# Local attention heads: the next job's first convolution laid between the logit turns, the softmax cut in three pieces

## The reference, cut to what matters

```
qkv = _conv1x1(xn, qkv_w, qkv_b).reshape(Bx, 3, HEADS, HD, Hx, Wx)
q, k, v = (qkv[:, 0], qkv[:, 1], qkv[:, 2])
...
qk = jnp.concatenate([(q * scale).reshape(Bx * HEADS, HD, Hx, Wx), k.reshape(Bx * HEADS, HD, Hx, Wx)], axis=1)
attn = jax.lax.conv_general_dilated(qk, dm_w, (1, 1), [(PAD, PAD), (PAD, PAD)], ...) + dm_b[None, :, None, None]
attn = attn.reshape(Bx, HEADS, K, Hx, Wx)
attn = attn + rel_bias.T[None, :, :, None, None]
attn = jax.nn.softmax(attn, axis=2)
...
out = jnp.einsum('bnckhw,bnkhw->bnchw', patches, attn).reshape(Bx, C, Hx, Wx)
```

## Time and profile before

| what | value |
|---|---|
| median of three runs | 5192.02 us |
| profiled execution: device time | 5200.72 us |
| profiled execution: span of the trace | 5198.9 us |
| PE busy | 4499.5 us (87%) |
| VectorE busy | 4251.0 us (82%) |
| POOL busy | 4077.5 us (78%) |
| ScalarE busy | 3168.0 us (61%) |
| first and last convolution matmul of the heads | 1308.2 to 2381.7 us |

### The profile page before, as it was taken

One profiled execution on the slowest core, in us unless ns is written; L12 is line 12 of the kernel. 1 busy time (PEld: TensorE's weight loads), 2 busy tenths in 40 slices (PEclk: granted clock), 3 DMA queues, 4 the chain that ended last, 5 costly groups with the idle time before them and its releaser, 6 DMA issues. The chain is left out here.

```text
span 5198.9 us, 68471 instructions
## 1 busy us (share of the span) xinstructions
PE 4499.5 (87%) x15210; PEld 2107.5 (41%) x15210; DVE 4251.0 (82%) x3462; ACT 3168.0 (61%) x6678; POOL 4077.5 (78%) x1926
## 2 busy tenths in 40 slices
PE   7998797986999999993788888889898888889897
PEld 2333463641666666662542323233232323232222
DVE  3776555554289999999559999999999999999995
ACT  5886565542011111110569888888888888888886
POOL 2544555544288988989659999999999999999993
PEclk9998998987999999996889999999999999999998
DMA  2000111327777777872428888788888888878883
GB/s 55 1 1 10 50 33 52 79 62 228 164 142 139 150 145 146 149 141 43 104 62 198 199 201 202 191 201 201 199 202 199 201 198 199 202 195 203 200 201 95
DMA packets 389221, 733.15 MB, mean 141 GB/s; under 512 B 78332, under 2 KB 119464, under 8 KB 375912
## 3 DMA queue, kind: packets, MB, share of 16 engines
q1 hardware_dynamic: 388968, 730.30, 60.3%
HBM read 594.31 MB, written 82.32 MB: 130 GB/s over the span
## 5 line engine op out<-in xcount | busy, mean ns | idle before, releaser
L2256 POOL TENSOR_TENSOR l_hc<-l_h,l_c_rep 128x1024 f32<-128x1024 f32 x768 | 1800.9, 2383 | 22.4 <-DVE l_h L2327 19.8
L1434 POOL TENSOR_TENSOR front<-l2b_v,front 128x1568 f32<-128x1568 f32 x276 | 936.9, 3463 | 235.4 <-ACT front L1395 119.0
L2327 DVE TENSOR_TENSOR_SCAN l_h<-l_p,l_h,l_bu 128x1024 f32<-128x1024 f32 x448 | 1026.3, 2328 | 5.3 <-ACT l_bu L2164 3.5
L2011 PE MATMUL l_p<-l_stacked,l_pick 96*128 96x512 f32 x1536 | 560.1, 446 | 224.3 <-DVE l_h L2327 204.9
L1482 DVE TENSOR_REDUCE l2b_osum<-front 128x32 f32<-128x1568 f32 x384 | 665.6, 1780 | 62.9 <-POOL front L1434 59.1
L2245 POOL TENSOR_TENSOR l_pool_bu<-l_du_rep,l_b_sb 128x1024 f32<-128x1024 f32 x256 | 610.7, 2386 | 39.7 <-DMA l_du_rep<-du_scratch 39.6
L2311 DVE TENSOR_TENSOR l_bu<-l_du_rep,l_p 128x1024 f32<-128x1024 f32 x512 | 610.8, 1193 | 25.7 <-DMA l_du_rep<-du_scratch 20.1
L1387 ACT ACTIVATE l2b_logits<-l2b_conv,l2b_this_b 98x512 f32<-98x512 f32 x96 | 66.1, 689 | 862.6 <-PE l2b_conv L1352 862.6
L2011 PEld LDWEIGHTS l_p<-l_stacked,l_pick 96*128 96x128 f32 x1536 | 242.8, 190 | 803.8 <-DVE l_h L2327 645.0
L2020 PE MATMUL l_p<-l_hc,l_y_pick 128*32 128x512 f32 x3072 | 522.1, 606 | 5.4 <-POOL l_hc L2256 5.4
L2327 DVE TENSOR_TENSOR_SCAN l_h<-l_p,l_h,l_pool_bu 128x1024 f32<-128x1024 f32 x224 | 523.2, 2336 | 3.6 <-ACT l_pool_bu L2164 2.3
(11 more groups left out here) (271 smaller groups left out, 8952.9 us busy)
## 6 DMA issues: line engine op xcount, KB each, us to landing
l_du_rep<-du_scratch SPq DMA_DIRECT2D x1536, 256.0 KB, 4.9
l2b_img_high<-qkv_scratch SPq DMA_DIRECT2D x192, 306.2 KB, 5.7
l2b_img_low<-qkv_scratch SPq DMA_DIRECT2D x192, 306.2 KB, 9.6
l_stacked<-l_parts SPq DMA_DIRECT2D x512, 96.0 KB, 3.3
l2b_v<-v_scratch SPq DMA_DIRECT2D x192, 152.0 KB, 6.4
qkv_scratch<-l2a_strip SPq DMA_DIRECT2D x32, 840.0 KB, 5.2
du_scratch<-l_du SPq DMA_DIRECT2D x128, 192.0 KB, 2.1
l_w_raw<-L_w_sed SPq DMA_DIRECT2D x32, 576.0 KB, 3.8
```

The lines of the kernel that those rows point to most:

```text
L1434: return eng.tensor_tensor(dst.rearrange("q x (dy dx) -> q x dy dx", dx=WIN), window, attn_half[:, :, unit % 2].rearrange("q x (dy dx) -> ...
L2011: pe.matmul(p_da[p % 2][:, e, :], pick[:, GRP[i] % (Q // DL), :], stacked[:, par, GRP[i] * DL // Q, :], start=True, stop=True).then_inc(s_ ...
L2256: pool.tensor_tensor(hc[:, slot:slot + 2, :], h[:, 2 * p:2 * p + 2, :], c_rep[:, par, :].unsqueeze(1).to_broadcast([128, 2, N]), ALU.mult) ...
L2327: dve.tensor_tensor_scan(flat(h[:, 2 * p:2 * p + 2, :]), flat(p_da[p % 2]), flat(of), state, ALU.mult, ALU.add).then_inc(s_h, 1)
```

## The change

`conv` is cut into three calls of a new `conv_pass`, one for each run of 14 matmuls. On PE the first chunk of job j+1 leaves the start of the next pass of the loop and goes between job j's turns: run 0, turns 0 to 2, run 1, turns 3 to 5, run 2, turns 6 and 7. Chunk 0 of job 0 goes ahead of the loop. The wait for the last logits stands behind run 0. On VectorE the softmax front is cut in the same three pieces, before units 26, 27 and 28. Nothing else is changed: SP, ScalarE and POOL run the same order of work, and no instruction of work is added or taken away.

```diff
-    SOFTMAX_AT = 26
+    SOFTMAX_AT = {26: (0, 1, 2), 27: (3, 4, 5), 28: (6, 7)}
...
+            PRODUCTS = ((0, 0), (1, 0), (0, 1))
+
+            def conv_pass(j, n, at, first=False):
+
+                b, ch = n // CHUNKS, n % CHUNKS
+                if at == 0:
+                    if ch == 0:
+                        pe.wait_ge(s_img[b % 2], 16 * 2 * SHIFTS * (B // 2) * j + 16 * 2 * SHIFTS * (b // 2 + 1))
+                    if not first:
+                        pe.wait_ge(s_log, j * JCHUNKS + (n - 1))
+                w_part, x_part = PRODUCTS[at]
+                for g in range(GROUPS):
+                    for dx in range(WIN):
...
+                if at == len(PRODUCTS) - 1:
+                    mm.then_inc(s_conv, 1)
+
             def conv(j, n, first=False):
...
+                for at in range(len(PRODUCTS)):
+                    conv_pass(j, n, at, first)
...
             def job(j, head, half, has_next, has_second):
                 first = isinstance(j, int) and j == 0
-                for n in range(JCHUNKS):
+                for n in range(1, JCHUNKS):
                     conv(j, n, first=first and n < 2)
-                pe.wait_ge(s_log, j * JCHUNKS + JCHUNKS)
-                for g in range(TURNS):
-                    turn(j, half, g, first=first and g < 3)
+                for at, groups in enumerate(SOFTMAX_AT.values()):
+                    if has_next:
+                        conv_pass(j + 1, 0, at)
+                    if at == 0:
+                        pe.wait_ge(s_log, j * JCHUNKS + JCHUNKS)
+                    for g in groups:
+                        turn(j, half, g, first=first and g < 3)
 
             pe.wait_ge(s_w, 64)
             pe.wait_ge(s_bias, 3)
+            conv(0, 0, first=True)
             all_jobs(job, pe)
...
-            def softmax(j, half):
-                for g in range(TURNS):
+            def softmax(j, half, groups):
+                for g in groups:
...
-                    if unit == SOFTMAX_AT and has_next:
-                        softmax(j + 1, 1 - half)
+                    if unit in SOFTMAX_AT and has_next:
+                        softmax(j + 1, 1 - half, SOFTMAX_AT[unit])
...
-            softmax(0, 0)
+            softmax(0, 0, range(TURNS))
```

More of the change, by code:

```diff
@@ L1340, in _ @@
         def _(pe):
-            def conv(j, n, first=False):
[L1343 to L1355, removed]
+            PRODUCTS = ((0, 0), (1, 0), (0, 1))
[9 more added lines that the diff above has]
+                    for dx in range(WIN):
+                        row = 2 * CP * ch + SHIFTS * g
+                        mm = pe.matmul(p_conv[n % 2][:], w_conv[w_part][:, g, dx, :],
+                                       img[x_part][:, b % 2, row:row + 2 * CP - 1:2, dx:dx + W],
+                                       start=(at == 0 and g == 0 and dx == 0),
+                                       stop=(at == len(PRODUCTS) - 1 and g == GROUPS - 1 and dx == WIN - 1))
+                if at == len(PRODUCTS) - 1:
+                    mm.then_inc(s_conv, 1)
+            def conv(j, n, first=False):
+                for at in range(len(PRODUCTS)):
+                    conv_pass(j, n, at, first)
             def turn(j, half, g, first=False):
```

## The result

| | before | after |
|---|---|---|
| median of four runs | 5191.84 us | 5227.28 us |
| profiled execution: device time | 5200.72 us | 5224.72 us |
| profiled execution: span | 5198.9 us | 5222.9 us |

The ratio is 1.0061, with a 95% interval of 1.0048 to 1.0075: 35.4 us slower between the medians. The prediction said 5223 us, between 5202 and 5252, and slower with a chance of 0.84.

What follows compares the result with a forecast made beforehand. PE's cycle set the pace, with the chain through SP's queue about 1 us from binding. Cycles +15.3, first job -2.4, clock +15, pieces +3 gave +31 us on 5192.0: 5223 us, range 5202 to 5252.

Steps and rivals of the forecast that it cites:

- The image's chain: VectorE, POOL, store, then load: image b=2 still lands 48.0 us after a job's first turn, unmoved by the change.
- PE's earlier arrival: PE reaches chunk 4 at 41.2 us after the first turn, was 49.2, so it newly waits 6.8 us for b=2.
- The cycle: First turn to next first turn: 91.85 us a job against 90.07, before clock and pieces are added.
- The clock: PE's granted clock falls in the idle ahead of chunk 4: 1.5 us a job, bounds 0 and 2.35.
- The pieces: VectorE's softmax cut in three meets the turns within 0.1 us: 0.3 us a job charged.
- VectorE's idle before its first maximum: Sign in the trace after: this idle up from 1 to 2 us to 4 to 5.
- First job: Job 0 has no store in the queue, so job 1 starts its turns 2.4 us early.
- Image b=0 as next in line: Load needed at 88.5 us after the first turn, estimated to land at 87: nothing charged, but next in line.
- the faster one: Rival: image b=2 in time for chunk 4, VectorE with POOL bind at 88.6 us a job: 5175 us, chance 0.08.
- Cold runs between the turns: Rival: transposes keep PE's clock low through runs 1 and 2, 3.36 us longer each: about 5290 us, chance 0.08.

Runs made afterwards that it cites:

- e3: Changed kernel with VectorE's softmax front whole again, in one piece before unit 26, PE's order as changed: 5258.14 us, ratio 1.0120 to the kernel before.
- e1: Changed kernel with the finished job's output store put behind image b=2 in SP's queue instead of ahead of it: 5205.08 us, ratio 1.0015 to the kernel before.
- e6: Changed kernel with SP's loads in the order their gates open, b=2 ahead of v's second half and the store, b=0 ahead of v's first half: 5174.69 us.
- e9: e6 with one move taken back, image b=0 behind v's first half again: 5218.94 us, ratio 1.0048 to the kernel before.
- e2: Kernel before the change with the output store put behind image b=2 in SP's queue: 5194.27 us, ratio 0.9996.
- e4: Changed kernel with 32 extra matmuls, result unused, on PE ahead of chunk 4's wait for image b=2: 5215.70 us, ratio 1.0035 to the kernel before.

## Why the prediction was right, point by point

- **The image's chain** (put at 48.0 us after the first turn, unmoved): chunk 4 started on it between 47.6 and 49.0, on average 48.3. Shown by the trace, by e3, which lengthens the chain by 2.9 us and the cycle with it, and by e1 and e6, which cut it and get 22 and 53 us back.
- **PE's earlier arrival** (41.2): 40.6, since three turns within the runs take 1.26 us of PE's time and not 1.6. The wait is thus 7.7 us on average instead of 6.8, the landing being 0.3 later as well; the earlier arrival makes the cycle no longer, as only the landing counts.
- **The cycle** (91.85 plus 1.8 for clock and pieces, 93.65): 94.0 us, from (2317.85 - 1471.48)/9 with the trace's first turns of jobs 1 and 10. From the first turn of job 1 to that of job 11 it is 938.4 us against 900.66: +37.7, where the sum had +33.3. The 4.4 us between them are the clock +6.4, the chain +2.8, the pieces -3 and the rest -1.8: the errors partly cancel, and that 5223 came so near 5227 is to that extent luck. The single distances are 92.9 to 95.5 us, a little wider than the 93 to 94 forecast.
- **The clock** (1.5 us a job, bounds 0 and 2.35): the term that was mis-sized most. Chunk 4 takes 1.4 to 2.8 us more than 10.07 after its wait, 2.1 on average over the ten. I had scaled it from the turns, in which PE was partly busy; a bare idle of 7 us costs more. The average lies within the upper bound, four single jobs over it. No row that I had read showed such an idle, but the trace of the kernel before has one, at the very first chunk of the heads, and it would have given 12.24 - 10.07 = 2.2:

```profile
1308.21 5.67 PE L1352 MATMUL l2b_conv<-l2b_img_high,l2b_w_conv_high 128*98 128x512 f32 x14 [33.13 <-DMA l2b_img_low<-qkv_scratch]
...
1320.45 3.54 PE L1352 MATMUL l2b_conv<-l2b_img_high,l2b_w_conv_high 128*98 128x512 f32 x14
```

- **The pieces** (0.3): from job 1 on VectorE never waits for piece 2 or 3; they cost nothing that I can see. e3 gives the price of leaving them out, 31 us.
- **VectorE's idle before its first maximum** (forecast 4 to 5): 3.8 to 7.1 us in jobs 2 to 11, 5.4 on average, which is the cycle of 94.0 less VectorE's own 88.6.
- **First job** (-2.4): first turn of job 0 to that of job 1 84.2 us instead of 89.85, from the first chunk on -2.8.
- **Image b=0 as next in line**: right, and it decided e9 and part of e1. In e9 it lands at 87.2 to 88.2, against an estimate of 87 made for the changed kernel.

Of the rivals, the faster one (the image in time, then 88.6 us a job and 5175 us) is what e6 made: 5174.7. It was priced rightly and given little, since nothing in the change touched the queue. Cold runs between the turns did not come: the granted clock is 1.00 over the 10.25 us of turns and runs. The Trainium skill's rule in "TensorE: Matmul & The Clock Gate", Part 4, that transposes don't count as PE activity like other matmuls, is not refuted by that, as this stretch is not of transposes alone. Where the changed kernel has turns with nothing between them, in job 11, the granted clock is 0.62 (2409.87 to 2420.00 us, PE busy for 5.99 of 10.13): that fits the rule and does not prove it, since PE also waits there.

## What to carry to other kernels

Before moving work ahead on one engine, find for each thing that it waits for whether that moves too: here a load was issued only when its queue reached it, and what stood ahead of it waited for a third engine. A change that takes 5 us a job from the busiest engine and still makes the job 4 us longer can be right and need only a second edit: here the loads had to stand in the order in which their gates open. Issuing the store from another engine's queue would take it out of the image's way too; no run tries it. In a cycle of several engines, write down every loop with its length (here PE's after the change 84.8, VectorE's 88.6, PE's before it 90.1, and the one through SP's queue 91.9 us without the clock's part); the longest one after the edit is the result.

## What the runs showed of the hardware that I had not expected

- SP went round its loop in e1 with v's small packets in flight, and its next DMA was issued 8.65 us late (1690.27 after 1681.62), in jobs 6 and 8 9.0 and 9.1 us late; in the job between two rounds the gap was 0.3 us. In e2, with the same queue, the gap is 8.6 to 9.2 us in the same three jobs and 4.1 to 5.3 in the jobs between them, where the image waits for chunk 1. The DMA view of 1700 to 2060 us names queue 14, the instructions' own, in e1 and in every other kernel with an edited queue (10 packets each in e2 and e6 to e9); in the kernel before, the changed kernel, e3 and e4 it has data alone. Here e1, then the kernel before:

```profile
q14 instruction: 8, 0.07, 0.1%
```
```profile
q1 hardware_dynamic: 24081, 52.30, 78.5%
```

  That the loop's code is loaded anew each round and waits behind the data fits, but no run isolates it. In e6 queue 14 is in use as well, but there the round ends after image b=1, some 24 us before the next DMA may go, and no issue comes late.
- A wait of 7 to 8.4 us ahead of dense matmuls cost 2.1 us on average through the granted clock, and 32 extra matmuls ahead of it made the program 11.6 us faster (e4).
